# Attention output: one product for two heads, after adding the context halves and scaling them by spread row sums

## The reference

```python
q = (hidden_states @ q_proj_w.T)                       # 16 heads, 128 + 64 dims each
kv = _rmsnorm(k_pass_lat, kv_a_ln_w) @ kv_b_proj_w.T   # keys and values from a latent of rank 64
scores = jnp.einsum('bhqd,bhkd->bhqk', q, k) * scaling
scores = jnp.where(causal[None, None], scores, NEG)
probs = jax.nn.softmax(scores.astype(jnp.float32), axis=-1)
out = jnp.einsum('bhqk,bhkd->bhqd', probs, v)
return out.reshape(b, s, H * V_DIM) @ o_proj_w.T
```

## Time and profile before

| | us |
|---|---|
| median of 3 runs | 816.39 |
| lowest, highest run | 814.26, 821.08 |
| span of the profiled execution, first to last instruction | 851.6 |
| attention slots in it, first to last context copy | 81.0 to 409.7 |

### The profile page before, as it was taken

How to read it: one execution, slowest core, us unless ns; L and a number is a source line. 1 busy time by engine, 2 the same in 40 slices (tenths; PEclk the granted TensorE clock), 3 DMA queues, 4 the chain that set the end, 5 groups by cost and what they waited for, 6 DMA issues and landing times.

```text
span 851.6 us, 16159 instructions
## 1 busy us (share of the span) xinstructions
PE 786.6 (92%) x4635; PEld 660.7 (78%) x4635; DVE 556.9 (65%) x1423; ACT 394.8 (46%) x898; POOL 271.2 (32%) x357
## 2 busy tenths in 40 slices
PE   8998999999899999999879998899999799999957
PEld 7887877778787887777677877788897688888746
DVE  4324778877778787777345555468856387778536
ACT  1334656656565666655123343323333266666411
POOL 2004445534333232222345545524415100000241
PEclk9999999999999999999889999999999999999979
DMA  7449950000000000073176999687621335555321
GB/s 212 102 107 384 406 198 34 34 27 27 21 27 28 20 21 14 27 240 135 51 230 184 323 319 296 213 288 257 246 99 69 106 112 150 149 149 153 95 69 49
DMA packets 62881, 120.74 MB, mean 142 GB/s; under 512 B 18272, under 2 KB 32864, under 8 KB 62688
## 3 DMA queue, kind: packets, MB, share of 16 engines
q1 hardware_dynamic: 51824, 95.41, 35.2%
q0 software_dynamic: 7680, 21.51, 7.0%
q10 hardware_dynamic: 3312, 3.02, 1.0%
HBM read 76.13 MB, written 43.78 MB: 141 GB/s over the span
## 4 chain that ended last, share of the span: by engine, by line
PE 65%; DVE 11%; issue 11%; ACT 4%; POOL 3%; another core or an unknown queue 3%; DMA 2%; DVEq 0%; SPq 0%; ACTq 0%; POOLq 0%
PE scores L1627 9%; PE scores L1625 8%; PE scores L1626 8%; PE scores L1849 5%; PE acc_ps L2035 4%; PE misc_ps L1755 3%; PE probsT_ps L1762 3%; PE probsT_ps L1740 3%; PE misc_ps L1753 3%; DVE xT_lo L1096 3%; PE scores L1859 3%; PE acc_ps L1740 2%; PE probsT_ps L1979 2%; DVE neg_max L1090 2%
## 5 line engine op out<-in xcount | busy, mean ns | idle before, releaser
L826 ACT ACTIVATE area<-scores,neg_max 128x128 f32<-128x128 f32 (+7 forms) x128 | 94.9, 742 | 87.7 <-DVE neg_max L1090 85.5
L1090 DVE TENSOR_REDUCE neg_max<-scores 128x1 f32<-128x128 f32 (+7 forms) x128 | 95.8, 750 | 22.1 <-PE scores L1712 20.8
L708 POOL DMA_INDIRECT xe_d<-x_rows,send_i x64 | 64.1, 1001 | 55.5 <-ACT x_rows L850 38.5
L738 POOL DMA_INDIRECT ye_d<-area,home_i x64 | 61.4, 959 | 58.7 <-issue 28.6
L1849 PE MATMUL scores<-area 128*96 128x128 f32 x512 | 69.1, 279 | 2.1 <-issue 1.3
L1625 PE MATMUL scores<-kT_hi,weff_hi 128*128 128x512 f32 (+3 forms) x172 | 66.8, 388 | 0.9 <-ACT area L803 0.4
L1849 PEld LDWEIGHTS scores<-area 128*96 128x96 f32 x512 | 60.5, 166 | 5.2 <-issue 2.7
L1627 PE MATMUL scores<-kT_hi,weff_lo 128*128 128x512 f32 (+3 forms) x172 | 61.7, 359 | 0.0
L1626 PE MATMUL scores<-kT_lo,weff_hi 128*128 128x512 f32 (+3 forms) x172 | 61.5, 358 | 0.0
L696 POOL CAST weff_hi<-area 128x256 fp32r<-128x256 f32 x42 | 17.0, 406 | 136.5 <-PE scores L1712 88.8
L1755 PE MATMUL misc_ps<-xT_lo,xT_hi 128*128 128x512 f32 x144 | 58.4, 406 | 2.2 <-DVE xT_lo L1096 2.1
(11 more groups left out here) (290 smaller groups left out, 2081.4 us busy)
## 6 DMA issues: line engine op xcount, KB each, us to landing
area<-w SPq DMA_DIRECT2D x23, 512.0 KB, 4.0
area<-gate_up SPq DMA_DIRECT2D x24, 384.0 KB
xe_d<-area SPq DMA_DIRECT2D x8, 1088.0 KB, 11.3
ye_d<-area SPq DMA_DIRECT2D x8, 1024.0 KB, 16.7
area<-w SPq DMA_DIRECT2D x8, 1024.0 KB, 7.2
area<-ye_d SPq DMA_DIRECT2D x15, 512.0 KB, 5.2
area<-xe_d SPq DMA_DIRECT2D x28, 272.0 KB
area<-down SPq DMA_DIRECT2D x24, 192.0 KB
```

The source lines that it names most:

```text
L826: act.activation(row_of(n)[:, 0:L], score_bank(n)[:, 0:L], ACT.Exp, bias=neg_max[:, n % 4:n % 4 + 1], accum_out=rsum[:, s, k:k + 1]).then_ ...
L1090: dve.tensor_reduce(neg_max[:, n % 4:n % 4 + 1], score_bank(n)[:, 0:(n // HEADS + 1) * P], AX.X, ALU.max, negate=True).then_inc(max_ready, 1)
```

## The change

- The context halves are added before the output product (`sum_context`, DVE, two instructions a group on 64 partitions by 256 columns): heads 0 and 2 of the group end in partitions 0 to 63 of `ctxS`, heads 1 and 3 in partitions 64 to 127.
- `wvo` holds for a pair of heads the two 64 x 256 matrices, one above the other. Two accumulating products a group (`output(g)`) give the sum of four heads, and one addition a group (`add_out`) brings it into `x1`.
- As heads are summed inside the product, the inverse row sums are applied before it, along the columns. `spread_shares(g)` on SP writes the group's 128 x 4 inverse sums, transposed, to `shares_d` in DRAM and reads them back twice, spread over 64 partitions each; `share(g)` on POOL multiplies (in slot 1, two groups later).
- `invert(G)` moves from slot (G+1, 1) to (G, 3). The output moves to slot 2 of group g+2 (g+3 for g = 0, 1); one tenant a group.
- The first context product of a group waits for `sum_context` of the one before, where it waited for `copy_ctx`.
- On SP the zeroing of `ye_d` and `xd_d` is spread over groups 8 to 21, one transfer after each `spread_shares`; half of the first experts' weights is loaded after group 30's shares, the rest after those of group 31.

```diff
+        ctxS, shares = cutA3(3, HID), cutA3(3, HID)
...
+        def out_slot(g):
+            return g + (2 if g >= 2 else 3)
...
-                if spot % 2 and 0 <= G - 2:
-                    tenants.append(("out", QUAD * (G - 2) + spot // 2))
+                if spot == 5:
+                    tenants += [("out", g) for g in outs_at(G)]
...
+            def spread_shares(g):
+
+                sp.wait_ge(rinv_done, g + 1)
+                sp.dma_start(shares_d[g].rearrange("a b p -> p (a b)"), rinv[:, g % 3, :],
+                             allow_slow_non_contiguous=True).then_inc(ld_kv, 16)
+                if g >= 3:
+                    sp.wait_ge(ctx_shared, g - 2)
+                sp.wait_ge(ld_kv, 16 * (g + 2))
+                for b in range(2):
+                    sp.dma_start(shares[b * RANK:(b + 1) * RANK, g % 3, :].rearrange("p (a n) -> p a n", a=2),
+                                 bass.AP(shares_d.tensor, (g * QUAD + b) * P, [[0, RANK], [2 * P, 2], [1, P]])).then_inc(ld_xT, 16)
...
+            for g in range(GROUPS):
+                spread_shares(g)
+                if 0 <= g - 2 * SETS < ZEROINGS:
+                    zero(g - 2 * SETS)
+                if g == GROUPS - 2:
+                    sp.wait_ge(q_split, TILES * PAIRS)
+                    load_first(0)
+                    load_first(4)
...
+            def share(g):
+
+                pool.wait_ge(ctx_summed, 2 * g + 2)
+                pool.wait_ge(ld_xT, 16 + 32 * (g + 1))
+                pool.tensor_tensor(ctxS[:, g % 3, :], ctxS[:, g % 3, :], shares[:, g % 3, :], ALU.mult).then_inc(ctx_shared, 1)
...
             def copy_ctx(G):
                 act.wait_ge(ctx_step, blocks_to(G + 1))
-                if G >= 2:
-                    act.wait_ge(out_ready, QUAD * (G - 1))
-                act.copy(ctxT[:, G % 2, :], ctx_ps[:]).then_inc(ctx_copied, 1)
+                act.copy(ctxT, ctx_ps[:]).then_inc(ctx_copied, 1)
...
+            def sum_context(g):
+
+                dve.wait_ge(ctx_copied, g + 1)
+                if g >= 3:
+                    dve.wait_ge(out_ready, g - 2)
+                for b, other in ((0, 1), (1, 0)):
+                    mine_, its = (slice(k * RANK, (k + 1) * RANK) for k in (b, other))
+                    dve.tensor_tensor(ctxS[mine_, g % 3, :].rearrange("p (a n) -> p a n", a=2),
+                                      ctx_ps[mine_, :].rearrange("p (a b n) -> p a b n", a=2, b=2)[:, :, b, :],
+                                      ctxT[its, :].rearrange("p (a b n) -> p a b n", a=2, b=2)[:, :, b, :],
+                                      ALU.add).then_inc(ctx_summed, 1)
...
-                dve.scalar_tensor_tensor(x1[:, t, :], out_of(n), rinv[:, s, k:k + 1], x1[:, t, :] if h else x_in[:, t, :],
-                                         ALU.mult, ALU.add).then_inc(out_read, 1)
+                dve.tensor_tensor(x1[:, t, :], out_of(g), x_in[:, t, :] if first else x1[:, t, :],
+                                  ALU.add).then_inc(out_read, 1)
...
-                behind = n - 1 - 2 * QUAD
-                if 0 <= behind < TILES * HEADS:
-                    add_head(behind)
+                if i == 0 and 0 <= G - 2 < GROUPS:
+                    sum_context(G - 2)
+                if i == QUAD - 1:
+                    for g in outs_at(G):
+                        add_out(g)
...
-                        pe.wait_ge(ctx_copied, G)
+                        pe.wait_ge(ctx_summed, 2 * G)
...
+            def output(g):
+                pe.wait_ge(ctx_shared, g + 1)
+                take_seat("out", g)
+                m = g % SETS * 2
+                for a in range(2):
+                    last = pe.matmul(out_of(g), ctxS[:, g % 3, a * P:(a + 1) * P], wvo[:, (m + a) * HID:(m + a + 1) * HID],
+                                     start=a == 0, stop=a == 1)
+                last.then_inc(out_ready, 1)
```

More of the change, by code:

```diff
@@ L94, in build @@
         weff_lo = sb("weff_lo", [P, 2, HC, P], f32r)
-        wvo = cutA3(HEADS * HID)
+        wvo = cutA3(PAIRS * HID)
+        ctxS, shares = cutA3(3, HID), cutA3(3, HID)
         qT = area1
@@ L401, in route_at, with outs_at @@
             return route_places.get((G % SETS, place)) if SETS + 2 <= G < GROUPS else None
+        def out_slot(g):
+            return g + (2 if g >= 2 else 3)
+        def outs_at(G):
+            return [g for g in range(GROUPS) if out_slot(g) == G]
         tenants = []
@@ L408, in build @@
                 tenants += [("block", b) for b in blocks_at(G - 1, spot)]
-                if spot % 2 and 0 <= G - 2:
-                    tenants.append(("out", QUAD * (G - 2) + spot // 2))
-        tenants += [("out", QUAD * (GROUPS - 1) + i) for i in range(QUAD)]
+                if spot == 5:
+                    tenants += [("out", g) for g in outs_at(G)]
+        tenants += [("out", g) for g in outs_at(GROUPS + 1)]
         tenants += [(what, TILES - 1) for what in route_places.values()]
@@ L418, in build @@
         LENT = pT + [acc, half[3]] + half[0:3]
-        long_rows = seat("out", TWO_OUTS)
+        long_rows = seat("block", blocks_to(SHORT // QUAD - 2))
         tail = seat("block", blocks_to(GROUPS - 1))
@@ L515, in _, with zero @@
                              zero_rows[:, 0:2 * ROW].unsqueeze(1).broadcast_to([P, 4, 2 * ROW])).then_inc(rows_zeroed, 16)
-            for b in range(SLOTS // T, 2 * SLOTS // T):
-                sp.dma_start(ye_d[b * T:(b + 1) * T, :].rearrange("(p b a) n -> p b (a n)", p=P, b=2),
-                             zero_rows[:].unsqueeze(1).broadcast_to([P, 2, T])).then_inc(zeroed, 16)
-            for b in range(0, BLOCKS * P, T // 2):
+            def zero(j):
+                b = j + SLOTS // T
+                if b < 2 * SLOTS // T:
+                    sp.dma_start(ye_d[b * T:(b + 1) * T, :].rearrange("(p b a) n -> p b (a n)", p=P, b=2),
+                                 zero_rows[:].unsqueeze(1).broadcast_to([P, 2, T])).then_inc(zeroed, 16)
+                    return
+                b = (j - SLOTS // T) * T // 2
                 n = min(T // 2, BLOCKS * P - b)
@@ L540, in _ @@
             sp.wait_ge(zeroed, 16 * ZEROINGS)
-            sp.wait_ge(q_split, TILES * PAIRS)
-            for e in range(0, IN_ADVANCE, 4):
-                sp.dma_start(first_gu[:, e:e + 4], gate_up0[:, e:e + 4]).then_inc(ld_first, 16)
-                sp.dma_start(first_dn[:, e:e + 4, :], down0[:, e:e + 4, :]).then_inc(ld_first, 16)
+            for e in range(8, IN_ADVANCE, 4):
+                load_first(e)
             sp.dma_start(w_c, w_in).then_inc(ld_wc, 16)
@@ L719, in pool_slot @@
                     split_q(n // 2 + 3)
+                if i == 1:
+                    for g in outs_at(G):
+                        share(g)
                 t, at = divmod(n - 2 * HEADS, HEADS)
@@ L792, in _ @@
             act.activation(sq[:], banks[1][:].rearrange("p (t n) -> p t n", t=TILES)[:, :, 0:RANK],
[L793 removed]
+                           ACT.Square).then_inc(kv_ready, 1)
             def weff_copy(h, u):
@@ L1053, in wvo_copy @@
                 hold(dve, wvo_ps, 2 * m + 2)
-                dve.tensor_copy(wvo[:, bass.ds(2 * m * HID, 2 * HID)], misc[:]).then_inc(wvo_done, 1)
+                for b in range(2):
+                    ins = dve.tensor_copy(wvo[b * RANK:(b + 1) * RANK, bass.ds(m * HID, HID)],
+                                          misc[b * RANK:(b + 1) * RANK, b * HID:(b + 1) * HID])
+                ins.then_inc(wvo_done, 1)
             kv_ps = banks[1][:].rearrange("p (t n) -> p t n", t=TILES)
-            dve.wait_ge(sq_done, 1)
+            dve.wait_ge(kv_ready, 2)
             dve.tensor_reduce(ms[:], sq[:], AX.X, ALU.add).then_inc(dve_step, 1)
@@ L1234, in dve_slot @@
                     go_on()
-                if i == 1 and 0 <= G - 1 < GROUPS:
-                    invert(G - 1)
+                if i == QUAD - 1 and G < GROUPS:
+                    invert(G)
                 if routed and at == (3, 1):
@@ L1755, in context @@
                 pe.matmul(ctx_ps[:], latent[:, k, :], pT_lo[b % 3], start=False, stop=k == tile_of(G)).then_inc(ctx_step, 1)
-            def output(n):
-                G, i = divmod(n, QUAD)
-                pe.wait_ge(ctx_copied, G + 1)
-                take_seat("out", n)
-                h = n % HEADS
-                pe.matmul(out_of(n), ctxT[:, G % 2, i * P:(i + 1) * P], wvo[:, h * HID:(h + 1) * HID],
-                          start=True, stop=True).then_inc(out_ready, 1)
+            def output(g):
[6 more added lines that the diff above has]
+                last.then_inc(out_ready, 1)
             def transpose_x1(t):
@@ L1812, in pe_slot @@
                 steps(G, 2 * i + 1)
-                if 0 <= G - 2 < GROUPS:
-                    output(QUAD * (G - 2) + i)
+                if i == 2:
+                    for g in outs_at(G):
+                        output(g)
             head_slots(pe_slot)
```

40 lines of the change are left out of this document (21 added, 19 removed).

## The result

The changed kernel takes 911.9 us (908.12 to 913.75), the kernel before beside it on the same chip 814.73 us (813.24 to 821.08): a ratio of 1.118, interval 1.115 to 1.121. The forecast was 803.4, the range 782 to 815. It is slower by 97 us, on the side to which the prediction gave 0.13, and by far more than either of its slower rivals.

What follows compares the result with a forecast made beforehand. The prediction took PE to set the pace, with DVE close behind. Removed work 22.0, seats 0, order of the sum -2 and first shares -7 gave 13.0 us off 816.4: 803.4 us, range 782 to 815.

Steps and rivals of the forecast that it cites:

- (c): Inverse sums' DRAM store and loads: 2.4 us each, about 6 with issue, hidden within one and a half group lengths.
- (C): Rival: stores queue behind zeroings, shares late in groups 8 to 21, 26 us added, 829 us; chance 0.08.
- 22.0: Attention stage: gain in us from removed work, midway between PE's 28.8 and DVE's 15.2.
- rival (B): Attention loop through PE, ACT, DVE is the pace; removed PE time becomes waits, 813 us; chance 0.15.
- DVE, 475 ns for a half sum: Each new half sum takes as long as an old addition; DVE relieved by 15.2 us in all.
- Order of the sum (2 us): `sum_context` heading DVE's slot 0 delays the next group's first context product: 2 us lost, bounds 0 and 15.2.
- seats (0): Outputs take one seat a group instead of four, easing transposes' waits: gain between 0 and 10.2 us, taken as 0.
- weights (hidden): Later loads of the experts' weights, 4.6 MB in 16 us, stay hidden with some 6 us to spare.
- wvo copies: Copy of `wvo` becomes two instructions on half the partitions: zero, or 3.6 us if cover were missing.
- The first shares: Start of the attention stage: first shares come late, PE stands 6 us, clock falls; 7 us lost, between 0 and 14.
- The tail, 0: From last context copy to last addition: 4.9 us before, 4.8 after, plus 0.3 for POOL's sends; zero in sum.
- (D): Rival: PE's clock falls to 1.2 GHz repeatedly in the short groups, 25 us added, 828 us; chance 0.05.

Runs made afterwards that it cites:

- e1: Changed kernel without the store of inverse sums and the waits for it, loads reading rows of x (wrong numbers): 810.61 us, ratio 0.993.
- e3: Changed kernel with the 2 KB store as 128 pieces of 16 B, same addresses, other order of the sums: 817.64 us, ratio 1.002.
- e4: Changed kernel with all zeroings issued ahead of the first store instead of one a group: 934.15 us in one run.
- e5: Changed kernel with the store's 512 pieces of 4 B each 512 B apart, loads reading x: 813.91 us in one run.
- e12: Kernel before without the odd heads' output products and additions (that part of the result missing), nothing added: 812.99 us, ratio 0.997.
- e0_before: Kernel before, unchanged, run again for a profile near its median: 813.83 us.
- e13: Kernel before with the row maximum taken over half of the columns: 803.79 us, ratio 0.986.
- e14: Kernel before with half-column row maximum and without the odd heads' output products and additions: 793.11 us, ratio 0.971.
- e10: Changed kernel, PE spreading the sums instead of DRAM transfers, a group's two products in two slots, addition heading the next group's slot 0: 832.19 us.
- e16: e1 with the row maximum taken over half of the columns: 797.52 us, ratio 0.980.

## Why the prediction was wrong

Point by point, with the prediction's own steps:

1. **(c), the shares' way through DRAM: the step that failed.** It took 2.4 us for "the store is in 4-byte pieces, which no row shows", from a load of 64 KB in pieces of 256 B. It takes 10.4 us from issue to the next issue, 15 at the end. So what (c) calls hidden, and puts into the sum as nothing, was not: by e1 the step is worth 101 us, of which the form of the store is 94 (e3). The bound of "one and a half group lengths" was also the wrong one: SP handles one group after the other, store, landing, loads, so what counts is one whole turn of its list against one group. The prediction has this turn, for the first shares alone and as 3.6 us, with the same 2.4 in it. By its own bound 10.4 + 1.3 + 2.8 = 14.5 us for store, issue and loads are too long where it allows 9.7, in the short groups, and would fit in the long ones. An unknown cost was given the value of the nearest row and no upper end; the range had no room for it.
2. **(C), shares late in groups 8 to 21.** The form was right (share late, store too slow for the group), the cause not: e4 has no zeroing in the loop and takes 394.9 us from the first loads to the last, against 398.8; e3 has them and is as fast as before. 26 us were forecast for eight groups; `share` waited for its loads in 25, 176 us in all.
3. **The Trainium skill's rule** ("DMA: Bandwidth & Descriptors", Specifications: pieces below 512 B are written by read-modify-write) was cited and put out of the sum, for want of a price. It pointed at the right transfer. But the size of the pieces alone, as the rule has it, doesn't tell the time: e5's pieces are of 4 B too, and land in 1.9 us. What costs is pieces of 4 B side by side. That this is repeated read-modify-write of the same memory would fit the table of distances, but no row shows the memory at work.
4. **22.0, what the removed work is worth.** 3.5 us by e12, 5.8 by e1 with all that the change adds. This is rival (B), 813 against e1's 810.6: "the loop of scores, maximum, exponential, transposes and copies is the pace, and the removed PE time turns into waits of PE". It got 0.15 because "PE waits so little". A PE at 95% was taken for a PE without slack; by e12 13 of the 28.8 us never left the busy time and 11 more became waits, so that share said little about what removed work gives. The weight loads' share was the better sign, 77% in e0_before (250.57 of 323.7). The Trainium skill ("Perfetto Trace Analysis", Identifying the Most-Contended Engine) says that matmul busy time is a poor measure, and that TensorE's headroom is judged by the share of peak arithmetic done and the busy share of the weight loads; the trace agrees as to the sign of the second. Taken as a price it fails too: that the weight loads leave 23% free doesn't say that half the products are worth 3.5 us.
5. **DVE, 475 ns for a half sum.** It took 422, and the new addition 425 instead of 475 (after: 96 x 0.42 = 40.5 us, so 20 and not 15.2 us relieved). Right in kind; it changed nothing in the outcome.
6. **Order of the sum (2 us), seats (0), weights (hidden), wvo copies.** e1 holds all of them and lies 6 us below before; none was measured by itself. The weights' loads did matter in another way: they hold up the last store.
7. **The first shares, 7 us.** PE stood for 13.1 us before the first output, released by `share`, where two gaps of 3 were forecast; in e1 2.9 remain. By the same error as in 1.
8. **The tail, 0.** 12.1 us, for the same cause, behind four loads of weights. The prediction counted six hand-overs of the tail and not the store and loads among them.
9. **(D), the clock.** It was at 0.64 of full speed from 81 to 131 us and 0.78 from 131 to 205 where it had been 0.97 and 1.00, and is 1.00 over the stage of e1, so it is a consequence of PE's standing. That it cost little of its own is argued, not measured: up to 393.71 SP's list was the pace, and after that the clock is 1.00.

What stays open: e13 and e14 show that DVE's maximum and PE's products share the pace, not which hand-over holds PE up; why the split order costs 7.7 us (e10); whether what the change adds eats what it removes (e16); and what the memory does with pieces side by side.

## What to carry to other kernels

A transfer of 2 KB is not small if it is in pieces of 4 B laid side by side: price it from a row with the same piece and the same spacing, or leave the range open upwards. Transfers that one queue handles in turn, each waited for, form a loop of their own; compare one turn of it with the time between two turns, and look where its last turn ends. And in a stage where PE reads 95% busy beside a second engine at 78%, removed work can give a fifth of what added work costs: 3.5 us for 28.8 us of products less (with their additions), 36 for 57.6 us more, 0.12 against 0.62 us for each us of PE's work.

## What the runs showed that I had not expected

The same 2 KB from the same 128 partitions took 10.4 us from the store's issue to that of its loads as 512 pieces 4 B apart, 2.9 at 16 B, 2.2 at 64 B and 1.9 at 512 B, and 2.2 as 128 pieces of 16 B without room between (this case's medians of 32). While such a store is under way the transfer engines look idle. This is the view of the transfers from 96.6 to 105 us of the changed kernel, in 40 slices of 0.21 us, each digit the engines' busy share in tenths:

```profile
DMA  1333358410000000000000000000000000000000
GB/s 49 85 93 110 98 97 73 29 1 0 0 0 0 0 0 0 0 0 0 0 0 0 0 0 0 0 0 0 0 0 0 0 0 0 0 0 0 0 0 0
DMA packets 816, 0.13 MB, mean 16 GB/s; under 512 B 560, under 2 KB 816, under 8 KB 816
```

The 816 packets are the 528 of the store and the 288 of the two loads before it. All are over after some 2 us, and six more pass until SP, which waits for the landing, goes on. A queue's busy share says nothing of such a wait; only the distance from its issue to its landing, or to who waits for it, does.
